# A message-passing kernel whose 34 edge tiles are cut into blocks of 11, 13 and 10 instead of 10, 14 and 10

## What is computed

```python
x1 = x_nodes[src].reshape(-1, N_SEG, EXTENT)
x2 = x_edges.reshape(-1, N_SEG, EXTENT)
i1, i2, i3 = (path_indices[:, 0], path_indices[:, 1], path_indices[:, 2])
contrib = path_coeffs[None, :, None] * x1[:, i1, :] * x2[:, i2, :]
edge_out = jnp.zeros((x2.shape[0], N_SEG, EXTENT), x_nodes.dtype).at[:, i3, :].add(contrib)
out = jnp.zeros((n_nodes, OP_SIZE), x_nodes.dtype).at[dst].add(edge_out.reshape(-1, OP_SIZE))
```

## Time and profile before

| what | value |
|---|---|
| median of 3 runs | 279.0 us (278.96 to 279.01) |
| the profiled execution | 279.03 us, its span 277.2 us |
| PE busy | 266.0 us (96%) |
| DVE busy | 225.2 us (81%) |
| ACT busy | 165.1 us (60%) |
| POOL busy | 63.1 us (23%) |
| chain that ended last | PE 78%, DVE 9%, ACT 7% of the span |
| granted TensorE clock | full, over the whole span |

### The profile page before, as it was taken

The page is one execution under the profiler, slowest core; times in us unless marked ns, Lnnn a source line. Parts: engine busy times, 40 slices in busy tenths (PEclk is TensorE's granted clock), DMA queues, the critical chain, the costliest instruction groups (busy, mean ns, idle before and its releaser), DMA issues.

```text
span 277.2 us, 5688 instructions
## 1 busy us (share of the span) xinstructions
PE 266.0 (96%) x1657; PEld 185.5 (67%) x1657; DVE 225.2 (81%) x662; ACT 165.1 (60%) x335; POOL 63.1 (23%) x52
## 2 busy tenths in 40 slices
PE   6899999999999999999999999989999999999995
PEld 4566698886443899997678777755666654478631
DVE  5977565199657999999999999999999987746371
ACT  6920541010527899946778786599988629432350
POOL 4000060060006545204769990000000000000000
PEclk9999999999999999999999999999999999999999
DMA  6799990000014657734150002024544348000002
GB/s 184 246 411 405 446 395 17 0 2 1 9 42 127 174 156 233 243 88 111 40 156 0 2 8 70 2 69 134 172 150 146 115 134 320 2 0 2 2 0 76
DMA packets 12448, 33.91 MB, mean 122 GB/s; under 512 B 3329, under 2 KB 3330, under 8 KB 12162
## 3 DMA queue, kind: packets, MB, share of 16 engines
q1 hardware_dynamic: 10338, 26.73, 27.1%
q0 software_dynamic: 2080, 6.82, 8.3%
HBM read 32.50 MB, written 1.05 MB: 121 GB/s over the span
## 4 chain that ended last, share of the span: by engine, by line
PE 78%; DVE 9%; ACT 7%; issue 3%; DVEq 1%; DMA 1%; ACTq 0%; SPq 0%
PE psum L1317 14%; PE psum L1267 12%; PE psum L1221 10%; PE psum L1320 8%; PE psum L1245 5%; PE psum L1250 4%; PE psum L1392 3%; DVE big L1011 3%; PE psum L1405 3%; PE psum L1164 3%; PE psum L1150 2%; PE psum L1273 2%; PE psum L1308 2%; PE psum L1173 1%; PE psum L1415 1%
## 5 line engine op out<-in xcount | busy, mean ns | idle before, releaser
L454 POOL DMA_INDIRECT big<-xn_rows,big x26 | 51.3, 1974 | 54.5 <-DMA xn_rows<-xn 23.5
L589 ACT ACTIVATE prod<-edges,coef_b 128x320 f32 (+1 forms) x77 | 43.0, 593 | 10.4 <-PE psum L1320 8.8
L1267 PE MATMUL psum<-big,dst_oh 128*128 128x512 f32 x104 | 48.8, 593 | 0.0
L1001 DVE TENSOR_TENSOR prod<-big,prod 128x320 f32<-128x320 f32 (+1 forms) x77 | 40.5, 527 | 0.4 <-DVE big L972 0.2
L1317 PE MATMUL psum<-prod,ident 128*128 128x128 f32 x160 | 32.0, 294 | 0.6 <-DVE prod L1001 0.5
L1317 PEld LDWEIGHTS psum<-prod,ident 128*128 128x128 f32 x160 | 24.4, 190 | 10.0 <-issue 9.1
L1221 PE MATMUL psum<-edges,big 128*128 128x256 f32 x128 | 28.3, 380 | 0.0
L1267 PEld LDWEIGHTS psum<-big,dst_oh 128*128 128x128 f32 x104 | 18.0, 191 | 13.5 <-issue 13.4
L1221 PEld LDWEIGHTS psum<-edges,big 128*128 128x128 f32 x128 | 24.1, 190 | 3.5 <-issue 0.3
L1011 DVE TENSOR_TENSOR big<-big,prod 128x64 f32 (+2 forms) x80 | 26.3, 328 | 0.1
L589 ACT ACTIVATE xparts<-edges,coef_b 128x320 f32 (+1 forms) x45 | 24.1, 584 | 0.9 <-PE psum L1317 0.9
(11 more groups left out here) (214 smaller groups left out, 500.8 us busy)
## 6 DMA issues: line engine op xcount, KB each, us to landing
big<-in_w SPq DMA_DIRECT2D x3, 2048.0 KB, 15.7
edges<-in_f SPq DMA_DIRECT2D x11, 512.0 KB, 3.5
edges<-in_edge SPq DMA_DIRECT2D x1, 3584.0 KB, 23.9
edges<-in_edge SPq DMA_DIRECT2D x1, 2560.0 KB, 23.6
edges<-in_edge SPq DMA_DIRECT2D x5, 512.0 KB
edges<-in_f SPq DMA_DIRECT2D x1, 2560.0 KB, 10.0
big<-in_gnn_w SPq DMA_DIRECT2D x1, 1024.0 KB, 6.6
xs<-in_x SPq DMA_DIRECT2D x1, 512.0 KB, 3.3
```

Source lines behind the costliest of these rows:

```text
L454: nc.gpsimd.indirect_dma_start(out=x1g[b % 2][:, i, :], out_offset=None, in_=xn_rows, in_offset=bass.IndirectOffsetOnAxis(ap=idx_i[:, 0, F ...
L589: nc.scalar.activation(slot(n)[:, 0:BLOCKS[b], :], segment(edges[:, FIRST[b]:FIRST[b] + BLOCKS[b], :], single_column(words, p)), ACT.Copy, ...
L1001: nc.vector.tensor_tensor(v, segment(xg[:, 0:tiles, :], first_column(words[b], p)), v, ALU.mult).then_inc(mults, 1)
L1267: last = mm(bank[2 + h], dst_oh[:, n % DR, h * P:(h + 1) * P], tile_sums(b, t), start=False, stop=False)
```

## The change

The first block gets one tile more, the second one fewer. `KEPT` stays 8, 6 and 4, so that VectorE adds 3, 7 and 6 tiles instead of 2, 8 and 6. The rooms follow from the same numbers; the sum of their sizes is the same. The second edit only names the end of a slice.

```diff
-    BLOCKS = [10, 14, 10]
-    FIRST = [0, 10, 24]
+    BLOCKS = [11, 13, 10]
+    FIRST = [0, 11, 24]
     KEPT = [8, 6, 4]
...
-        rest_sums = [sum_room[0][:, KEPT[0]:, :], sum_room[1], sum_room[0][:, KEPT[2]:, :]]
+        rest_sums = [sum_room[0][:, KEPT[0]:, :], sum_room[1], sum_room[0][:, KEPT[2]:BLOCKS[2], :]]
```

## The result

The changed kernel takes 284.4 us (284.28 to 284.66, 4 runs) against 279.0 us for the kernel before, timed beside it: a ratio of 1.0195, 95% interval 1.0182 to 1.0207. It is slower by 5.4 us. The forecast was 284.0.

The account below looks back on a forecast made before the run. VectorE was taken to pace the first two blocks, with TensorE nearly as slow in the second; the late boundary shifts the rest by 4.9 us: 279.0 + 4.9 = 283.9, with gather 284.0. Likeliest case (0.76) 283.2 to 284.9; range 281.9 to 286.0.

Parts of the forecast that it names:

- First block, +4.19 us: First block on VectorE: 32 more columns in multiply and add, 65.5 ns a path over 64 paths, +4.19 us.
- Third gather, +0.1 us: Before multiply 0: a third gather estimated to land at 90.35, nearly hidden; +0.1 us, bounds nothing to about 1 us.
- Second block, VectorE, -4.19 us: Second block on VectorE: 65.5 ns less a path, -4.19 us, so by itself ready for multiply 128 at 182.5.
- TensorE, 44.5 us from the first scatter to the end of the last: Second block on TensorE: 54 paths and 11 scatters from 137.98 take 44.5 us, ending at 182.5, without catching up.
- Clearing and one-hot copy, 3.12 + 0.31 us: Third block's start on ScalarE: clearing 3.12 us, one-hot copy 0.31, so scale 128 starts at 185.95, 4.9 us later.
- A wait of ScalarE of over 5 us ahead of the clearing: Sign expected if right: ScalarE waits over 5 us before the clearing, which starts near 182.5.
- Idle before multiply 128, about 4 us: Start of third block: VectorE idle some 4 us, multiply 128 at about 186.6 instead of 182.5, released by ScalarE.
- One scatter fewer in the third block gives nothing: Third block on TensorE: one scatter fewer, 1.72 us, gains nothing, as TensorE ends the block waiting for VectorE.
- nothing changes: Rival: the wait for the eleventh scatter stays hidden, leaving +4.19, -4.19 and +0.1: 279.1 us; chance 0.05.
- faster: Rival: TensorE carries the third block, so the scatter taken out there is worth 1.72 us: 277.3 us; chance 0.06.
- The first block hides part of its tile: Rival: something other than VectorE's columns paces the first block; at half of 4.19, 281.9 us; chance 0.05.
- Late gathers on top: Rival: third block's gathers hang on GpSimd until VectorE stops, delaying multiply 128: 285.7 to 288 us; chance 0.08.

Follow-up runs that it names:

- The new order of scatters: Changed kernel with the first block's kept tiles 4 to 7 scattered before 0 to 3, so clearing needs 7 scatters instead of 11: 282.03 us, ratio 1.0105.
- the shorter paths of TensorE: Changed kernel without the small matmuls that fill TensorE on every second path of the second block: 282.87 us, ratio 1.0136.
- the three causes taken away together: Changed kernel with kept tiles 4 to 7 scattered before 0 to 3, no filler matmuls, and only two gathers in the first block: 279.48 us, ratio 1.0016.
- one profiled execution: Changed kernel, kept tiles 4 to 7 scattered before 0 to 3, second block's bank copies behind scales 137 and 139: this execution 284.22 us; measured again 281.14.

## Why the prediction was right

The time lay 0.4 us above the forecast and within the likeliest case's own range. The mechanism is the one forecast: VectorE's work is conserved, TensorE stops catching up, and its last scatter of the first block's tiles arrives late at the clearing. By its steps:

- **First block, +4.19 us** from the price of a column: measured 4.00. The adds of 96 columns and multiplies of 352 cost what the slopes of the earlier trace rows say, less 3 ns a path.
- **Third gather, +0.1 us**: measured 0.96. This is the term of the sum that was mis-sized, and it makes up more than the whole error; the first block, 0.19 us shorter than forecast, happened to take some of it back. The forecast's last step, from 283.9 to 284.0, counts the 0.1 a second time, as it is already in the 4.9. The estimate took the landing time of a direct transfer of the same size, 2.0 us from issue. Multiply 0 starts 3.2 us after the third gather's instruction ends, at 88.34. The upper bound of about 1 us held. One gather fewer put 0.94 us of it back.
- **Second block, VectorE, -4.19 us**: it reached the end of the block as early as forecast, plus the late start, and then stood idle.
- **TensorE, 44.5 us from the first scatter to the end of the last**: measured 42.79 + 1.72 = 44.51. That TensorE would stop catching up was the core of the argument, and it has no wait for VectorE in that block. The step of 1.4 us of slack used up is in this number.
- **Clearing and one-hot copy, 3.12 + 0.31 us**: measured 3.13 and 0.30. The clearing starts at 183.23 instead of 182.5, by the 0.7 us that multiply 64 was later than forecast.
- **A wait of ScalarE of over 5 us ahead of the clearing**: measured 2.92, and 3.13 before. This sign did not come. It asked that ScalarE reach the clearing by about 177.5. But its scales wait for slots that TensorE frees, so ScalarE is late with TensorE too: scale 127, at 179.66, waited 0.94 us for the slot of path 115, and ScalarE was through at 180.31 instead of 174.77. The sum doesn't use this wait, and the scatter still came last, so the time did not suffer. But it is why the clearing began at 180.01, and not earlier, once the wait for the scatter was taken away.
- **Idle before multiply 128, about 4 us**: 4.16. **Multiply 134 near 191.6**: 192.33, released by ScalarE.
- **One scatter fewer in the third block gives nothing**: TensorE waits for VectorE at its end.

The rivals: *nothing changes* and *faster* asked for a hidden wait, which the rows at 183.23 and 187.47 rule out. *The first block hides part of its tile* asked for well under 4.19 us there, at half 2.1; the first block grew by 4.00. *Late gathers on top* did not come: the gathers of the third block did hang, one for 19.05 us, but the last began at 167.90, almost 20 us before multiply 128.

The experiments show the cause, and not the sum alone. The new order of scatters and the shorter paths of TensorE each take away part of the loss, the three causes taken away together give back all but 0.43 us, of which the moved one-hot copy is the larger part, and a second tile moved repeats the loss at about the size worked out. Not tried: a start of the first block's gathers ahead of the store of the rows that they read, which would be a race.

## What to carry to other kernels

When work is moved from one stage to another, add up each engine by stage, not over the kernel: VectorE's work broke even here, and it still lost 4.7 us at the boundary because TensorE, which took 0.76 us a path against its 0.87 in one stage, took 0.79 against 0.81 after a scatter had moved into that stage and columns out of it. An engine that trails another and catches up has slack, and the number to look for is where it catches up; once it no longer does, its lateness arrives at the next wait on something old, such as a room to be freed. Ask also what else the late engine paces: here TensorE held the scatter that ScalarE waited for and, by the slots, ScalarE itself. If one late engine is waited for at two places, take the second into the price of removing the first.

## What the runs showed of the hardware

**A gather's instruction on GpSimd can take many us beside a busy VectorE.** Most gathers take 0.94 to 1.11 us. In the changed kernel, in order of time:

```profile
94.00 9.78 POOL L454 DMA_INDIRECT big<-xn_rows,big  x1 [0.66 <-DVE xn L1001]
...
148.54 19.05 POOL L454 DMA_INDIRECT big<-xn_rows,big  x1 [1.06 <-DVE prod L1001]
```

VectorE in order of time, next to the end of the second of them:

```profile
166.19 0.58 DVE L1001 TENSOR_TENSOR src_t<-big,src_t 128x416 f32<-128x416 f32 x1
166.85 0.39 DVE L1011 TENSOR_TENSOR big<-big,src_t 128x224 f32 x1
```

The add starts 0.66 us after the multiply instead of the usual 0.50, and the gather ends at 167.59, 0.74 us after that. All six gathers over 3 us in the two kernels end in this way: in the changed one at 103.78, 123.64, 143.27 and 167.59, after pauses of VectorE before 103.16, 122.99, 142.56 and 166.85; in the kernel before at 139.09 and 165.39, after pauses before 138.34 and 164.61. Each end comes 0.6 to 0.8 us after the pause. That speaks for the two engines getting in each other's way, but the order of cause is open: the pause may let the gather through, or be what VectorE loses when the gather gets through. No run changed the pauses to test it, a busy VectorE alone does not do it (in the first block of the changed kernel seven gathers in a row from 104.09 take 0.94 to 1.02 us each), and one long gather, in the run with the scatters crowded to the front, ended at 162.92 with no pause ahead of it.

The Trainium skill (SBUF — State Buffer, Who interferes with whom) has a tensor_tensor with two inputs in SBUF contend with GpSimd's reads, which fits. It also infers that the generation of descriptors is not held up by a tensor_tensor. The 19.05 us speak against that only if descriptors are what these gathers were waiting to write; a gather also reads its offsets from SBUF, so its reads alone could be what is held up, and the rows don't tell the two apart.

**TensorE's clock fell after a short rest, in some kernels.** In the changed one TensorE worked at full clock up to 188.28, had nothing to do until 190.31, and then ran at half for about three us. By windows (us, busy time of each engine, granted clock, DMA share, GB/s):

```profile
189.00:190.00 1.00, 0.00 (x0) 0.00 (x0) 1.00 (x4) 1.00 (x4) 0.00 (x0) 1.00 0.00 0
190.00:191.00 1.00, 0.69 (x4) 0.33 (x5) 1.00 (x5) 1.00 (x3) 0.00 (x0) 1.00 0.00 0
191.00:192.00 1.00, 1.00 (x5) 0.55 (x4) 0.66 (x2) 1.00 (x3) 0.00 (x0) 0.50 0.98 274
```

That is 1.2 instead of 2.4 GHz. With one gather fewer the same rest of 2.03 us (187.36 to 189.39) was followed by half clock as well. But rests of 2.31 us without the fillers (before 188.68) and of 2.17 us with blocks of 12, 12 and 10 (before 197.22) left the clock at full, so the length of the rest alone doesn't decide. The half clock cost the end nothing, as TensorE caught up with VectorE by 230.49, and multiply 134 and the last multiply are late by the same 5.6 us.

**ScalarE was held up for several us in the first block of one profiled execution**, as in the row at 115.82 above. The gathers and edge loads move data all through it (292 GB/s from 104 to 108 us), but they do so in the later execution of the same program without a hold as well (286 GB/s). Two more executions took the same time as the held one and were not profiled, and none of the five later ones did. What held ScalarE stays open.
